# Reordered attention steps and a reordered entry in a two-layer local-attention kernel on one core

## What is computed

```
def _layer(x, ...):                       # twice, DEPTH = 2
    h = shift_token(x)                    # half of the features come from the token before
    q, k, v = split(h @ wqkv, 3)          # 8 heads of 64
    q = l2norm(q) * qs;  k = l2norm(k) * ksc
    q, k = rotary_xpos(q, k)
    o = local_attention(q, k, v)          # windows of 64 tokens, each sees itself and the one before; softmax
    x = x + o @ wo
    h = shift_token(x)
    h = (h - mean) / sqrt(var + 1e-5) * lg + lb
    a, g = split(h @ w1 + b1, 2)
    return x + (a * gelu(g)) @ w2 + b2
...
x = x + layernorm(linear_attention(layernorm(x)))
x = x + layernorm(layers(layernorm(x)))
```

## Time and profile before

| what | value |
|---|---|
| median of 3 runs | 471.43 us (471.33 to 474.74) |
| the profiled execution | 470.14 us |
| its span of instructions | 468.1 us |
| mean granted TensorE clock | 0.988 of full speed |
| PE busy | 418.4 us, 89% of the span |
| DVE busy | 355.0 us, 76% |
| ACT busy | 311.0 us, 66% |
| POOL busy | 259.5 us, 55% |

### The profile page before, as it was taken

How to read it: one execution, slowest core, us unless ns; L and a number is a source line. 1 busy time by engine, 2 the same in 40 slices (tenths; PEclk the granted TensorE clock), 3 DMA queues, 4 the chain that set the end, 5 groups by cost and what they waited for, 6 DMA issues and landing times.

```text
span 468.1 us, 13183 instructions
## 1 busy us (share of the span) xinstructions
PE 418.4 (89%) x4851; PEld 293.9 (63%) x4851; DVE 355.0 (76%) x738; ACT 311.0 (66%) x690; POOL 259.5 (55%) x241
## 2 busy tenths in 40 slices
PE   4998999779899999999879999899999999979992
PEld 2566666546667666766655566666767667665562
DVE  3688777877788888888854277888888888864557
ACT  3778868648577877887764247678778777756334
POOL 3578968879466567566650036565665665540003
PEclk9999999979999999999999999999999999999998
DMA  7910000000000000000000000000000000000003
GB/s 183 341 27 2 3 2 3 2 2 4 9 9 8 8 13 7 8 11 11 6 12 8 0 1 2 7 8 8 12 8 8 12 9 8 7 13 7 6 1 91
DMA packets 21038, 10.37 MB, mean 22 GB/s; under 512 B 13236, under 2 KB 20208, under 8 KB 20976
## 3 DMA queue, kind: packets, MB, share of 16 engines
q1 hardware_dynamic: 20400, 9.14, 7.2%
q10 hardware_dynamic: 576, 0.39, 0.3%
HBM read 6.38 MB, written 1.05 MB: 16 GB/s over the span
## 4 chain that ended last, share of the span: by engine, by line
PE 30%; DVE 27%; ACT 21%; issue 15%; POOL 2%; DMA 1%; SPq 1%; DVEq 0%; ACTq 0%; POOLq 0%
PE psum L604 25%; DVE ss L1823 8%; DVE neg_max L1840 7%; ACT sq L1313 6%; ACT qk_t L1332 5%; DVE probs L1847 4%; ACT probs_t L1345 3%; ACT probs L1338 2%; PE psum L863 2%; ACT ln_z L1367 1%; DMA hcat<-middle 1%; POOL qr L484 1%; DVE row_rec L1860 1%; DVE o_n L1867 1%; DVE x_in L1771 1%
## 5 line engine op out<-in xcount | busy, mean ns | idle before, releaser
L476 POOL TENSOR_TENSOR qr<-rot 128x1024 f32<-128x1024 f32 x32 | 75.8, 2369 | 75.7 <-issue 56.8
L604 PE MATMUL psum<-wqkv_sb,h_t 128*128 128x512 f32 x192 | 95.0, 605 | 0.6 <-ACT h_t L1306 0.6
L484 POOL TENSOR_TENSOR qr<-qr,inv 128x1024 f32<-128x1024 f32 x32 | 60.9, 1902 | 38.2 <-ACT inv L1324 38.2
L1823 DVE TENSOR_REDUCE ss<-sq 128x16 f32<-128x1024 f32 x32 | 39.0, 1219 | 29.5 <-ACT sq L1313 29.5
L1338 ACT ACTIVATE probs<-probs 128x512 f32<-128x512 f32 x64 | 40.4, 632 | 12.6 <-DVE probs L1847 11.9
L1847 DVE TENSOR_TENSOR probs<-psum,neg_max 128x512 f32<-128x512 f32 x64 | 44.0, 690 | 2.0
L604 PE MATMUL psum<-z_t,w_sb 128*128 128x512 f32 (+1 forms) x96 | 44.2, 593 | 0.0
L1840 DVE TENSOR_REDUCE neg_max<-psum 128x4 f32<-128x512 f32 x64 | 43.3, 681 | 0.7 <-PE psum L604 0.6
L604 PEld LDWEIGHTS psum<-wqkv_sb,h_t 128*128 128x128 f32 x192 | 32.1, 194 | 17.7 <-issue 16.8
L1815 DVE TENSOR_TENSOR rot<-psum,cos_t 128x1024 f32<-128x1024 f32 x32 | 38.8, 1213 | 4.6 <-PE psum L604 4.1
L863 PEld LDWEIGHTS psum<-consts,qr 128*128 128x128 f32 x256 | 30.2, 143 | 18.4 <-POOL qr L484 10.6
(11 more groups left out here) (148 smaller groups left out, 953.3 us busy)
## 6 DMA issues: line engine op xcount, KB each, us to landing
wqkv_sb<-in_L_ffn_wqkv SPq DMA_DIRECT2D x1, 1536.0 KB, 9.7
hcat<-middle SPq DMA_DIRECT2D x32, 32.0 KB
out_x<-pong SPq DMA_DIRECT2D x8, 128.0 KB, 2.0
hcat<-middle SPq DMA_DIRECT2D x32, 31.8 KB
x_in<-in_L_attn_x SPq DMA_DIRECT2D x2, 384.0 KB, 4.3
w_sb<-in_L_ffn_w SPq DMA_DIRECT2D x1, 682.0 KB
cos_base<-rotary_cos SPq DMA_DIRECT2D x1, 512.0 KB, 5.1
sin_base<-rotary_sin SPq DMA_DIRECT2D x1, 512.0 KB, 6.3
```

The lines of the kernel that those rows point to most:

```text
L476: pool.tensor_tensor(o, a, b[:, :, ::-1, :], ALU.add).then_inc(s["add_ready"], 1)
L484: pool.tensor_tensor(a, a, inv[:, :].unsqueeze(2).to_broadcast([P, 2 * AH, DH]), ALU.mult).then_inc(s["qr_ready"], 1)
L604: return pe.matmul(o, w, m, start=start, stop=stop, skip_group_check=skip)
L1823: dve.tensor_reduce(ss[:, :], sq[:, :].rearrange("p (h e) -> p h e", e=DH), AX.X, ALU.add).then_inc(s["ss_ready"], 1)
```

## The change

The steady step has another order on three engines, the transfer semaphore of `hcat` is split into one for even and one for odd tiles, the drain is adapted, and the hand-written entry has another order on four engines. No instruction of the computation is added or taken away.

- **DVE**: both `row_max` halves ahead of both `subtract_max` halves; `rotate` directly behind them; then `add_attention`, `normalise_z` (now of tile k-3, it was k-2), `stats_z`, `aggregate_z`; `row_reciprocals` moves from the head of the next step to a place between `sum_squares` and `bound_squares`.
- **ACT**: `ln_of_z` and `rstd_of_z` go from their place between the exponentials and `copy_qk_t` to behind `copy_v_cur`.
- **PE**: `transpose_probs` ahead of `project_o`, `weigh_values` ahead of `transpose_z`.

```diff
@@ transfers of hcat (SP) and their wait (DVE, stats_z) @@
-                                 ).then_inc(d["d_half"], 16)
+                                 ).then_inc(d[("d_even", "d_odd")[n % 2]], 16)
...
-                    wait(dve, d["d_half"], 48 * (N + 1))
+                    wait(dve, d[("d_even", "d_odd")[n % 2]], 48 * (N // 2 + 1))
@@ tensor: attn_step @@
                     staged(transpose_qk, k, par, 1)
+                    staged(transpose_probs, k, par, 0)
                     staged(project_o, k, par, -1)
-                    staged(transpose_probs, k, par, 0)
                     staged(project_v, k, par, 1)
+                    staged(weigh_values, k, par, 0)
                     staged(transpose_z, k, par, -3)
-                    staged(weigh_values, k, par, 0)
@@ scalar: attn_step @@
                     staged(exponentials, k, par, 0, 1)
-                    staged(ln_of_z, k, par, -2)
-                    staged(rstd_of_z, k, par, -2)
                     staged(copy_qk_t, k, par, 1)
                     staged(copy_probs_t, k, par, 0)
                     staged(squares, k, par, 2)
                     staged(copy_v_cur, k, par, 1)
+                    staged(ln_of_z, k, par, -2)
+                    staged(rstd_of_z, k, par, -2)
                     staged(copy_z_t, k, par, -3)
@@ vector: attn_step @@
                 def attn_step(k, par):
-                    staged(row_reciprocals, k, par, -1)
                     staged(normalise_o, k, par, -1)
                     staged(row_max, k, par, 0, 0)
+                    staged(row_max, k, par, 0, 1)
                     staged(subtract_max, k, par, 0, 0)
-                    staged(row_max, k, par, 0, 1)
                     staged(subtract_max, k, par, 0, 1)
+                    staged(rotate, k, par, 2)
+                    staged(add_attention, k, par, -1)
+                    staged(normalise_z, k, par, -3)
                     staged(stats_z, k, par, -2)
                     staged(aggregate_z, k, par, -2)
-                    staged(rotate, k, par, 2)
-                    staged(normalise_z, k, par, -2)
-                    staged(add_attention, k, par, -1)
                     staged(sum_squares, k, par, 2)
+                    staged(row_reciprocals, k, par, 0)
                     staged(bound_squares, k, par, 2)
@@ vector: drain @@
                     def last_outputs():
-                        row_reciprocals(last, last % 2)
                         normalise_o(last, last % 2)
+                        normalise_z(last - 2, (last - 2) % 2)
@@ tensor: attention_beside_last_pairs @@
                     key_values(7, 1)
+                    transpose_in(2, 0)
                     intra_outputs(7, 1)
...
                     scores(0, 0)
-                    pe.wait_ge(s["yn_ready"], NP)
-                    transpose_in(2, 0)
+                    project_out(7, 1)
                     project_qk(2, 0)
...
@@ vector: attention_beside_last_pairs @@
                     sum_squares(3, 1)
-                    stats_z(0, 0)
-                    aggregate_z(0, 0)
                     bound_squares(3, 1)
...
                     rotate(4, 0)
-                    normalise_z(0, 0)
+                    stats_z(0, 0)
+                    aggregate_z(0, 0)
                     add_attention(1, 1)
```

More of the change, by code:

```diff
@@ L539, in attention_beside_last_pairs @@
                     gate_values(7, 1)
+                    scale_qk(0, 0)
                     gate_o(7, 1)
-                    scale_qk(0, 0)
+                    rotate_add(1, 1)
                     add_y(6, 0)
-                    normalise_f(4, 0)
-                    rotate_add(1, 1)
                     scale_qk(1, 1)
@@ L547, in attention_beside_last_pairs @@
                     keep_values(0, 0)
+                    normalise_f(4, 0)
                     normalise_f(5, 1)
+                    rotate_add(2, 0)
+                    scale_qk(2, 0)
+                    normalise_f(6, 0)
                     add_y(7, 1)
[L550 to L553, removed]
                     mix_values(1, 1)
@@ L1064, in attention_beside_last_pairs @@
                     project_v(1, 1)
+                    weigh_values(0, 0)
+                    pe.wait_ge(s["yn_ready"], NP)
                     transpose_in(3, 1)
                     scores(1, 1)
-                    weigh_values(0, 0)
+                    transpose_in(4, 0)
                     project_qk(3, 1)
-                    transpose_in(4, 0)
                     transpose_o(0, 0)
                     transpose_qk(2, 0)
+                    transpose_probs(1, 1)
                     project_o(0, 0)
-                    transpose_probs(1, 1)
                     project_v(2, 0)
+                    scores(2, 0)
+                    weigh_values(1, 1)
                     transpose_in(5, 1)
-                    weigh_values(1, 1)
-                    scores(2, 0)
+                    project_qk(4, 0)
                     transpose_o(1, 1)
-                    project_qk(4, 0)
                     transpose_qk(3, 1)
@@ L1512, in attention_beside_last_pairs @@
                     copy_qk_t(2, 0)
+                    copy_probs_t(1, 1)
                     squares(3, 1)
-                    copy_probs_t(1, 1)
-                    copy_h_t(5, 1)
-                    ln_of_squares(3, 1)
-                    copy_v_cur(2, 0)
-                    inverse_norms(3, 1)
-                    ln_of_z(0, 0)
-                    rstd_of_z(0, 0)
+                    ln_of_f(7, 1)
+                    rstd_of_f(7, 1)
+                    ln_of_squares(3, 1)
+                    inverse_norms(3, 1)
+                    copy_v_cur(2, 0)
+                    exponentials(2, 0, 0)
+                    copy_h_t(5, 1)
                     copy_o_t(1, 1)
-                    exponentials(2, 0, 0)
                     exponentials(2, 0, 1)
@@ L1984, in attention_beside_last_pairs @@
                     sum_o(7, 1)
+                    state_1(7, 1)
+                    rotate(1, 1)
+                    scale_o(7, 1)
                     stats_y(6, 0)
                     aggregate_y(6, 0)
[L1987 to L1994 removed]
                     sum_squares(1, 1)
                     bound_squares(1, 1)
[L1997 removed]
+                    normalise_y(6, 0)
                     row_max(0, 0, 0)
```

229 lines of the change are left out of this document (113 added, 116 removed).

## The result

The changed kernel takes 484.23 us (median of 4 runs, 483.16 to 484.93); the kernel before, beside it on the same chip, 471.38 us. The ratio is 1.0267, with an interval from 1.0229 to 1.0305: slower by 2.7%. The profiled execution took 483.16 us, with a span of 481.2 and a mean granted clock of 0.993; that of before had a span of 468.1. The forecast was 482.

The account below looks back on a forecast made before the run. Bound before: a slackless ring through DVE and ACT, 9.04 us a step; after, `zn` held by POOL, 9.82. Terms 7.3 + 8.7 - 1.3 + 2.2 - 6.0 = +10.9 us on 470.14 give 481.0, median 482; range 472 to 490.

Parts of the forecast that it names:

- The hold: Steady step: `zn` on DVE, coming behind POOL's `rotate_add`, waits till it ends; step 9.82 us, 0.79 longer.
- The three holds of the earlier trace: Kernel before: two `ssc` and six `zn`-like instructions on DVE ended 0.03 to 0.08 us behind POOL's instruction.
- Rival A: Steady step: `zn` isn't held, PE bounds the step at 8.5 us; 453 us, faster by 4%; chance 0.14.
- the ring: Steady step, DVE and ACT waiting on each other: less 0.42 (ACT pair), 0.22 (maxima), 0.20 (reciprocal), 9.04 to 8.20 us.
- The table parts: POOL work that lengthened four first-layer steps by 0.35 us by holding `ssc`; now `ssc` comes after it, 4 x 0.35 less.
- Rival C: Steady step: table parts on POOL hold `zn` 0.73 longer in four steps (+2.9), entry gives nothing; 491 us; chance 0.08.
- The entry: Program start, hand-written order: two waits of DVE go, together 4.7 us; taken as -6, ends 0 and -9.
- The wait for the transfers: Entry: `stats_z` of tile 0 no longer makes DVE wait 2.39 us for the transfers.
- The other wait: Entry: `transpose_in` of tile 2 no longer waits on `yn_ready` of all pairs, removing DVE's 2.30 us for `project_qk`.
- The term for `ssc` of tile 2: Entry: `ssc` of tile 2 comes while POOL does `rotate_add` of tile 2; costs up to 1.2 us.
- The drains: End of each layer: `transpose_z` of tile 13 waits for its later `zn`; +1.1 us each, +2.2.
- One sign: Steady step: PE's idle time ahead of `transpose_o` was to rise from 0.6 to over 1 us.

Follow-up runs that it names:

- experiment 1: Changed kernel with `normalise_z` moved one line up on DVE, ahead of `add_attention`: 454.12 us, ratio 0.9643.
- experiment 2: Kernel before with two DVE lines swapped, `add_attention` ahead of `normalise_z`, nothing else: 498.61 us, ratio 1.0589.
- experiment 9: Changed kernel with POOL's `rotate_add` written as two instructions of eight heads each: 460.30 us, ratio 0.9751.
- experiment 10: Changed kernel with POOL's `rotate_add` written as four instructions of four heads each: 454.08 us, ratio 0.9615.
- experiment 7: experiment 1 with PE's steady order of the kernel before: 461.44 us, ratio 0.9766.
- experiment 8: experiment 1 with ACT's `ln_of_z` and `rstd_of_z` back behind the exponentials, a tile later: 456.79 us, ratio 0.966.
- experiment 4: Kernel before with only the changed kernel's entry on all engines, fitted to the old step: 468.79 us over 10 runs, ratio 0.9952.
- experiment 6: experiment 5 with the norm of z of tile 13 ahead of the row reciprocals in step k = 15: 450.32 us, ratio 0.9537.
- experiment 5: experiment 1 with `project_o` ahead of `transpose_probs` again in each layer's last attention step, k = 15: 451.44 us, ratio 0.9549.
- experiment 12: experiment 6 run again unchanged, on another chip: 450.49 us, ratio 0.9572.

## Why the prediction was right

**The hold.** The step went as the walk through it said, point for point. From the start of `o_n`, forecast and measured: `rotate` 3.17 and 3.16, its end 5.51 and 5.52, the addition on POOL 5.64 and 5.66, `add_attention` 5.82 and 5.80, `zn` 6.07 and 6.01, its end 8.10 and 8.11, the sum 8.44 and 8.45, the next `o_n` 9.82 and 9.81. It could be that close since all but one duration stood in the earlier trace rows, and the one that didn't, the held `zn`, has its end set by POOL. The three holds of the earlier trace rows were on other instructions; experiments 1, 2, 9 and 10 show that the mechanism is the same for `zn`.

**The bound without it.** Rival A put the step at 8.5 us, bound by PE, and the time at 453. Experiment 1 is that kernel: 8.47 and 454.12. The reading of the earlier trace rows, PE's own work from the step less its idle time, was right. So was rival A's condition; the time that it speaks of is reached once `zn` starts ahead of POOL.

**The gains of the ring.** The prediction gave 0.42 us to the pair on ACT and 0.42 to DVE, and nothing to PE's order, which it named for what it makes late. Experiments 7 and 8 put 0.36 us a step on PE's order and 0.1 on ACT's pair. With PE's old order and all the rest (experiment 7) the step fell from 9.03 to 8.83, by 0.20 of the 0.84 that the prediction takes off this ring. In the sum this made no difference, since the forecast step ran over POOL and not over this ring. As an account of where the change helps it was incomplete: `transpose_probs` moved up frees ACT of a wait.

**The table parts** on POOL no longer touch `ssc`, as the sum had it: the first layer's 11 steps grew by 7.5 and the second's by 8.7. Rival C's second loss did not occur. Once `zn` is free the hold on `ssc` is back: experiment 1 has 0.50 to 0.52 us for it in the same four steps, which are 0.19 longer than the others.

**The entry** gave 5.3 for a forecast of 6 in the profiles, but that is in part luck. The wait for the transfers is gone and `transpose_in` is earlier, as forecast. The other wait, DVE's 2.30 us for `project_qk` of tile 2, I had read as the price of waiting on `yn_ready`. PE's timeline of before shows what it was:

```profile
99.23 3.78 PE L604 MATMUL psum<-wqkv_sb,h_t 128*128 128x512 f32 x4 [0.64 <-ACT h_t L1306]
```

The same four pieces take 1.88 us in a steady step. The granted clock of before was 0.81 from 96 to 100 us and 0.50 from 100 to 104, behind idle time of PE, so by this some 1.9 of the 2.30 us belong to the half clock of that execution. After, the clock stayed at 1.00 from 84 to 125 us. Whether the new order keeps it there or this pair of executions differs by chance is not shown: experiment 4 gives 1.9 us in the median. The new entry moves many more lines than the two that the term was built on, and no run splits them. The term for `ssc` of tile 2, 1.2 us at most, was right: 1.44 us, where before it took 0.21. That `ssc` of tile 1 would take 1.88 for 1.57 and that of tile 3 0.74 for 0.16 it did not have.

**The drains** are the term that was mis-sized: +2.2 forecast, +3.6 measured. The prediction had named the norm of z alone, at 1.1 each. The first cost 0.9 and looks right, but experiment 6 puts only 0.4 of such a drain on the norm; the rest, some 0.5, goes by the comparison with experiment 5 (48.15 and 47.64 us) to the order of the last projection. The second cost 2.7. The projection behind the last probabilities was in the diff, and in the steady step I had used it, but the prediction did not ask what else PE has at k = 15. Experiment 5 shows that it costs 2 us where the clock falls.

**One sign was wrong.** The prediction named PE's idle time ahead of `transpose_o` as over 1 us; it is 0.57 there, less than before. The idle time is over 1 us for the step (0.46 + 0.57), but half of it stands ahead of `transpose_z`, which waits for the held norm first. In the whole program PE waits 12.9 us for `zn` (2.7 before) and 15.0 for `o_n` (14.5 before).

## What to carry to other kernels

Before an SBUF-to-SBUF tensor_scalar of VectorE is moved (the two forms seen here were f32), look up which GpSimd instruction runs at its new place: it costs what is left of that instruction, and here 0.2 us ahead or 0.35 behind was 30 us in 484. If the order can't be had, cut the long GpSimd instruction in pieces, which gave the same 30 us, at 0.42 us more for the addition itself. A new steady order should be walked through its last step too, where no next tile fills the gaps.

## What the runs showed of the hardware

The start that the profile gives is not the point that decides who is held: in experiment 2 `zn` starts 0.02 us ahead of POOL's addition in the trace and is held for the whole of it, while 0.21 us ahead (experiment 1) is enough.

The half clock (a granted clock of 0.50, 1.2 GHz) comes in some executions of the same kernel and not in others. Experiments 6 and 12 are one kernel. The entry by stretches of 4 us, first in the profile of experiment 12, then of experiment 6:

```profile
88.00:92.00 4.00, 3.49 (x14) 1.73 (x12) 3.97 (x7) 2.14 (x11) 3.90 (x3) 1.00 0.00 0
92.00:96.00 4.00, 2.35 (x32) 1.88 (x36) 3.93 (x7) 2.88 (x5) 3.46 (x2) 1.00 0.01 2
```

```profile
88.00:92.00 4.00, 3.54 (x36) 1.85 (x37) 3.26 (x8) 2.59 (x9) 3.93 (x4) 0.70 0.00 0
92.00:96.00 4.00, 3.62 (x20) 2.35 (x18) 3.10 (x5) 1.20 (x4) 1.86 (x2) 0.87 0.00 0
```

At 0.70 and 0.87 (and 0.72 from 70 to 76 us) `ss` of tile 4 comes at 125.30, at 1.00 at 121.93, and the spans are 452.0 and 448.6 us: the 3.4 us between them arose in the entry. That is more than several of the edits here are worth, so a difference of one profiled execution in the entry says little unless the clock beside it is the same. The 5.3 us of the changed entry is such a difference.
